# Gated cross-attention with an FFN on one core: where the FFN's weight pieces stand in the first batch

## The reference, cut to what matters

```python
q = _qdq(x) @ _qdq(wq).T + bq                  # x is layernorm(x); 16 heads of 32
kv = cond @ wkv.T + bkv
attn = softmax(einsum('bnhd,bmhd->bhnm', q, k) * scale)
o = einsum('bhnm,bmhd->bnhd', attn, v)
x = x + tanh(g_xattn) * (_qdq(o) @ _qdq(wp).T + bp)

def _quantized_matmul(x, w, scale):
    wq = w.astype(float8_e4m3fn).astype(x.dtype)
    return einsum('bsi,io->bso', x, wq) * scale
fuse = silu(_quantized_matmul(h, gate_w, gate_scale)) * _quantized_matmul(h, up_w, up_scale)
x = x + tanh(g_ffn) * _quantized_matmul(fuse, down_w, down_scale)   # h is layernorm(x)
```

## Time and profile before

| | |
|---|---|
| median of three runs | 920.49 us |
| the profiled execution | 921.14 us, its span 919.3 us |
| TensorE busy | 856.7 us, 93% |
| VectorE busy | 674.4 us, 73% |
| ScalarE busy | 554.2 us, 60% |
| POOL busy | 249.3 us, 27% |
| chain that ended last | TensorE 66%, VectorE 16%, issue 8%, ScalarE 7%, DMA 1%, POOL 1% |

### The profile page before, as it was taken

One profiled execution on the slowest core, in us unless ns is written; L12 is line 12 of the kernel. 1 busy time (PEld: TensorE's weight loads), 2 busy tenths in 40 slices (PEclk: granted clock), 3 DMA queues, 4 the chain that ended last, 5 costly groups with the idle time before them and its releaser, 6 DMA issues.

```text
span 919.3 us, 13602 instructions
## 1 busy us (share of the span) xinstructions
PE 856.7 (93%) x4968; PEld 316.1 (34%) x4976; DVE 674.4 (73%) x1306; ACT 554.2 (60%) x737; POOL 249.3 (27%) x236
## 2 busy tenths in 40 slices
PE   5989989997999999999899999999999989998998
PEld 2422212244433332224443332224433322234444
DVE  6888956988676779968676678986867778788222
ACT  5547978752456559873456649884356779862230
POOL 1145755875127600001017700002002210020230
PEclk9999999999899999999999999999999999999899
DMA  9334333221201133200111133300010023200001
GB/s 331 105 87 133 95 112 91 75 89 46 52 24 47 44 124 98 52 1 1 26 50 35 42 112 99 78 2 1 9 44 1 1 61 102 53 1 30 5 1 46
DMA packets 37251, 55.29 MB, mean 60 GB/s; under 512 B 8960, under 2 KB 15424, under 8 KB 37184
## 3 DMA queue, kind: packets, MB, share of 16 engines
q1 hardware_dynamic: 35264, 48.13, 18.4%
q0 software_dynamic: 1920, 6.29, 2.3%
HBM read 31.21 MB, written 4.19 MB: 39 GB/s over the span
## 4 chain that ended last, share of the span: by engine, by line
PE 66%; DVE 16%; issue 8%; ACT 7%; DMA 1%; POOL 1%; SPq 0%; ACTq 0%; DVEq 0%; POOLq 0%
PE ps L1389 32%; PE ps L1577 8%; PE ps L1540 7%; PE ps L1557 7%; DVE acc L1119 4%; ACT r L877 4%; PE ps L1512 4%; PE ps L1571 3%; PE ps L1585 1%; PE ps L1373 1%; DVE kst L1094 1%; DVE am L974 1%; DVE r L1261 1%; DVE vv L1186 1%; DVE xq L1094 1%
## 5 line engine op out<-in xcount | busy, mean ns | idle before, releaser
L877 ACT ACTIVATE r<-ps 128x1024 f32<-128x1024 f32 (+1 forms) x300 | 253.3, 901 | 59.6 <-PE ps L1540 57.2
L1094 DVE CUSTOM_DVE_ANT_0 kst<-ps,kst 128x512 f32<-128x512 f32 x192 | 124.5, 685 | 30.3 <-PE ps L1512 28.4
L1540 PE MATMUL ps<-qst,kst 97*128 97x512 f16 x512 | 138.7, 385 | 7.4 <-DMA qst<-crow 4.7
L1557 PE MATMUL ps<-r,vv 128*32 128x512 f32 x1024 | 138.1, 612 | 3.3 <-ACT r L877 3.2
L1119 DVE TENSOR_TENSOR acc<-acc,r 128x1024 f32<-128x1024 f32 x120 | 138.6, 1216 | 0.0
L834 ACT ACTIVATE kst<-ps 128x1024 f32<-128x1024 f32 x96 | 98.2, 1023 | 53.3 <-PE ps L1445 53.0
L1389 PE MATMUL ps<-xs,w_gate 128*128 128x512 f16 x384 | 92.6, 385 | 1.5 <-DVE xs L1306 1.5
L1389 PE MATMUL ps<-xs,w_up 128*128 128x512 f16 x384 | 91.2, 380 | 0.0
L1540 PEld LDWEIGHTS ps<-qst,kst 97*128 97x128 f16 x512 | 40.4, 97 | 145.0 <-ACT r L877 86.7
L932 ACT ACTIVATE qst<-ps,gs_c 128x512 f32<-128x512 f32 x48 | 33.0, 688 | 69.4 <-PE ps L1389 69.4
L1335 DVE SCALAR_TENSOR_TENSOR xq<-ps,us_c,qst 128x512 f32<-128x512 f32 x48 | 36.0, 749 | 52.3 <-PE ps L1389 52.3
(11 more groups left out here) (166 smaller groups left out, 1286.1 us busy)
## 6 DMA issues: line engine op xcount, KB each, us to landing
kst<-k_reg SPq DMA_DIRECT2D x192, 64.0 KB
qst<-q_reg SPq DMA_DIRECT2D x192, 32.0 KB
xs<-in_x SPq DMA_DIRECT2D x4, 1024.0 KB, 5.9
cf<-in_ctxT POOLq DMA_DIRECT2D x16, 256.0 KB, 3.5
xres<-in_x SPq DMA_DIRECT2D x3, 1024.0 KB, 5.1
out<-xres SPq DMA_DIRECT2D x12, 256.0 KB, 2.0
acc<-in_down_w SPq DMA_DIRECT2D x10, 256.0 KB, 2.7
vv<-in_wkvT SPq DMA_DIRECT2D x2, 1024.0 KB, 9.8
```

The lines of the kernel that those rows point to most:

```text
L877: nc.scalar.activation(prob[:, s:s + heads, :], ps[:, first_bank:first_bank + heads, :], ACT.Exp, scale=SCALE).then_inc(exp_done, 1)
L1094: ins = nc.vector.tensor_tensor_reduce(kept(b, n)[:, k, :], bank(PAIR + k), kept(b, n)[:, k, :], 1.0, -3.0e38, ALU.add, ALU.max, mx[:, g % ...
L1540: mm = nc.tensor.matmul(bank(first_bank + k), kst[0:97, g % 2, j + k, t * P:(t + 1) * P], qst[0:97, g % 2, j + k, :], start=True, stop=True)
L1557: mm = nc.tensor.matmul(ps[j * DH:(j + 1) * DH, O_BANK, :], vv[:, t, h * DH:(h + 1) * DH], prob[:, p_slot(b, u, j), :], start=(t == 0), st ...
```

## The change

Three pieces instead of six stand after value tiles: those after V2, V3 and V4. Units 15, 17 and 19 take one each, so that 27 stand in the units. Of the six late ones, the pair after V1 to V3 (L1275) moves behind the low half of K0. POOL follows: its chunks stand behind pieces 4, 6, ..., 18 instead of 7, 9, ..., 21, which from unit 16 on are earlier units (16, 18, 20 for 18, 21, 23); the inverse deviation stands behind piece 14, again that of unit 16; two pieces instead of four are rounded before the second inverse deviation, four after it. SP loads fewer pieces before each row and stack.

```diff
-W_EARLY, W_LATE = MT - len(EARLY_V), 6
+W_EARLY, W_LATE = 3, 6
-W_CHAIN = 4
-W_NONE = (3, 6, 9, 11, 13, 15, 17, 19)
+W_CHAIN = 2
+W_NONE = (3, 6, 9, 11, 13)
-W_VARIANCE = 16
+W_VARIANCE = 14
...
-W_AHEAD = {"keys1": 5, "shift0": 8, "queries1": 10, "shift1": 13, "stack2": 15, "shift2": 20, "stack3": 20,
-           "shift3": 24, "residual": 30}
-W_STACK = {2: (15, 16, 16, 16, 17, 17), 3: (20, 21, 21, 21, 21, 23)}
+W_AHEAD = {"keys1": 5, "shift0": 7, "queries1": 7, "shift1": 11, "stack2": 13, "shift2": 15, "stack3": 17,
+           "shift3": 23, "residual": 30}
+W_STACK = {2: (13, 13, 13, 13, 13, 13), 3: (17, 17, 17, 18, 19, 21)}
...
-            stack(qst, (qhi, qlo, qhi), 1, (9, 9, W_AHEAD["queries1"]))
+            stack(qst, (qhi, qlo, qhi), 1, (0, 0, W_AHEAD["queries1"]))
...
                 v_tile(a_full, a_count(f"V{n}"), A_BANK[f"V{n}"], a_free, n)
-                w_magnitudes()
+                if n < len(EARLY_V) + W_EARLY:
+                    w_magnitudes()
...
                 late_magnitudes(2)
                 next_v(1, 2, 3)
-                late_magnitudes(2)
...
                         k_low(b + 1, n, d_bank(b, f"K{n}"), d_free)
+                        late_magnitudes(2 * (n == 0))
```

## The result

The changed kernel takes **911.34 us** (median of 4 runs, 910.51 to 912.61); the kernel before, run beside it on the same chip, 920.83 (919.34 to 921.73). The ratio is 0.990, 95% interval 0.988 to 0.992: faster by 9.5 us. Forecast were 911.8 and a gain of 8.7. The profiled execution took 911.59 us, span 909.8, so it stands for the median. In the session of the first four experiments one run of the kernel before took 3535.54 us; it is left out of the medians and ratios here.

What follows compares the result with a forecast made beforehand. The chain is mostly TensorE's own work, so gains come only where it waits. Units 2.7 plus step 6.0 make 8.7 us off the median 920.49: 911.8 us, chance 0.60, range 908.0 to 916.0.

Steps and rivals of the forecast that it cites:

- Unit 16: Batch 0, unit 16: the row of maxima leaves SP at 127.3; TensorE's 3.87 us wait and 1.57 slow clock go, 5.44.
- Unit 24: Batch 0, unit 24: the row, ready at 159.4, lands just in time; TensorE's 0.86 us wait goes.
- Rival C: Slower: unit 24's row held behind piece 22's load, if POOL is 8.9 us later than summed; 921.5 or more, chance 0.04.
- Units 17 to 22: Batch 0: POOL is full, so new waits for maxima cost 4.0 us; units end 2.7 earlier, values' products included.
- The term of unit 21: Batch 0, unit 21: TensorE loses 0.7 us, carried on from the inverse deviation POOL delivers late in unit 17.
- rival A: Units 17 to 22: the new waits, hanging on one late deviation, don't come; gain 12.7, 907.8 us, chance 0.15.
- the 188.8 to 189 named as a sign: End of batch 0's units: they would be over near 188.8-189 us in the trace.
- Values' products: Batch 0: pieces 3, 4, 5 leave the places after V5, V6, V7; only V5's is on the path, gain 0.34 us.
- The step: Batch 0 to 1, first value product to matmuls behind K2's first difference: 46.5 us, 6.0 less than 52.49.
- The 1.0 for the key difference: Step, pieces 34 and 35 after K0's low half: the key difference TensorE wants is held by POOL, 0.4 to 1.0 us.
- The 0.2 for pieces 32 and 33: Step, after the normalisation: their 2.2 us stand against 2.03 us that VectorE waited for ScalarE, cost 0.2.
- from K3 on nothing changes: After the step: no change from K3 on, with TensorE continuous; no gain or loss summed there.

Runs made afterwards that it cites:

- the first four experiments: The units alone, the step alone, the row held and the early deviation: four edited kernels, measured 916.57, 915.25, 915.13 and 911.48 us.
- the row held: Changed kernel, but SP loads 17 pieces instead of 15 before the row of maxima of group 2; 915.13 us, ratio 0.9941.
- the early deviation: Changed kernel, with POOL computing the inverse deviation behind piece 13 (unit 15) instead of 14; 911.48 us, ratio 0.9907.
- the pair at K2: Changed kernel, with pieces 34 and 35 ahead of K2's low half instead of behind K0's; 909.52 us, ratio 0.9896.
- the units alone: Changed kernel, with pieces 32 and 33 back behind tiles V1 to V3 and four pieces before the second inverse deviation; 916.57 us, ratio 0.9957.
- the step alone: Kernel before, with only the pair after V1 to V3 moved behind K0's low half, two pieces before the second inverse deviation; 915.25 us, ratio 0.9938.
- the pieces spread: The pair at K2, plus pieces of units 17 and 19 moved to 11 and 13, deviation, chunks and SP's counts fitted; 908.18 us, ratio 0.9874.

## Why the prediction came out right

**Unit 16.** Right in cause and size. The row left at 127.80 for the 127.3 summed, TensorE did not wait, and the clock stayed up; the row held by two loads brings both back. Here the Trainium skill (TensorE: Matmul & The Clock Gate, "Part 1: The HAM clock gate") says that the slow clock is the default and that a monitor sets the clock by how busy TensorE has been of late. The trace agrees so far: after stops of 3.69 to 3.87 us at unit 16 the granted clock was 0.50 in all four profiles that have them. The length of a stop alone does not decide: after 1.76 us in the step it was 0.50 in one profile of five, after 2.55 us in the last batch in six of ten.

**Unit 24.** Right: no wait for its row, though its issue came at 161.00 where 159.4 was summed. TensorE was nearly as much later itself. It was close: the weight load of the first scores stood 0.8 us for the row, beside matmuls. Rival C needed far more.

**Units 17 to 22.** The mechanism was right, one size not. Summed were 2.1, 0.7 and 1.2; measured 2.02, 1.19 and 1.21. The term of unit 21 was too small by 0.5. I had derived it from the late deviation, and the held row and the early deviation both show that it does not hang on that. Nor do the three waits together hang on one late deviation, as rival A had it. All in all the stretch was 2.02 us shorter for the 2.7 forecast: 0.4 of the miss is the longer waits, the rest is not placed. With the start-up 0.37 us longer, the next batch's first product came at 190.17, not at the 188.8 to 189 named as a sign.

**Values' products.** Right: the wait behind V5 was 0.43 us for 0.76 (68.17 in the changed kernel), 0.33 for the 0.34 forecast.

**The step.** Right: 46.67 us for 46.5. The 1.0 for the key difference, which I took over 0.4 because a row showed VectorE holding POOL up, measured 0.84 (the stop of 1.76 less 0.92), and the pair at K2 gave 1.0 back. The 0.2 for pieces 32 and 33 is 0.3 at most: with the pair at K2 the step takes 45.66 us for the 45.33 of the next batch. By the Trainium skill (SBUF — State Buffer, "SBUF: two separate sides") the difference, with two inputs from SBUF, has to wait while an operation of POOL that reads SBUF holds the pair of ports that they share. The trace agrees: 1.05 us for 0.68 beside POOL's rounding, and POOL's next operation, at 235.74, took 1.60 us for 1.16.

**The last batch.** Not in the prediction at all. I wrote that from K3 on nothing changes, and the work did not; its time did. TensorE stands 2.55 us for the second normalisation in all ten profiles. In the kernel before the granted clock falls behind this stop, in the changed kernel it does not. The windows of before:

```profile
849.62:850.62 1.00, 1.00 (x6) 0.67 (x4) 1.00 (x3) 0.62 (x2) 0.00 (x0) 0.50 0.66 250
853.62:854.62 1.00, 1.00 (x3) 0.30 (x2) 0.00 (x0) 0.00 (x0) 0.00 (x0) 0.50 0.00 0
```

And of the changed kernel:

```profile
844.13:845.13 1.00, 0.79 (x4) 0.41 (x5) 0.06 (x1) 0.00 (x0) 0.00 (x0) 1.00 0.00 0
848.13:849.13 1.00, 1.00 (x7) 0.43 (x5) 0.61 (x1) 0.00 (x0) 0.00 (x0) 1.00 0.00 0
```

Without these 2.05 us the gain would have been 7.5 for the 8.7 summed: I was 1.2 too high on what I reasoned about (0.7 in the units, 0.2 in the step, and the start-up's 0.37), and the total hides it. That the forecast of 911.8 lies within 0.5 of the result is luck; with the last batch as before the time would have been near 913.4, still inside the range.

## What stays open

Why the last batch's clock goes one way in one kernel and the other way in the next. In ten profiles of eight kernels the work of that stretch is the same, and it takes 92.66 and 92.67 us (the kernel before, twice), 91.7 (the row held), 91.6 (the units alone), 91.5 (the step alone), 91.4 (the deviation early) and 90.6 (the changed kernel twice, the pair at K2, the pieces spread). What differs is the granted clock behind the 2.55 us stop. In the kernel before it is 0.50 from 850 to 855 us, through the turns of the normalised rows (L1373) and into the 192 matmuls. In the four with 91.4 to 91.7 us it is 0.50 in those turns alone, 16 matmuls that take 3.2 to 3.5 us where they take 1.94 at full clock, and the 192 take 41.60 as in the changed kernel. In the other four it does not fall. The chain of the units alone:

```profile
844.27 3.46 PE ps L1374 x16
849.21 41.60 PE ps L1390 x192
```

What decides it I can't say, and the time at which the stop comes does not alone: in the second profile of the changed kernel and in that of the early deviation the same piece of it begins at 833.31 and 833.24, and the stretches took 90.60 and 91.37. I did not try to shift that batch alone, and more profiles of one kernel would be needed to tell the kernel's part from chance.

## What to carry to other kernels

Where one queue issues everything in order, what stands ahead of an urgent transfer is part of its price: two loads too many cost 3.2 us in their own stretch and 3.8 in all. Before moving work to an engine that seems idle in a stage, add up all that its new neighbours already have there; the same 27 pieces made TensorE wait 4.4 us in one arrangement and 1.7 in another. And a gain from the clock can arrive in a stretch that the change never touches, so compare stretches, not totals.

## What I had not expected of the hardware

The lower clock of the last batch (granted 0.50) repeated in two profiles of each kernel: 92.66 and 92.67 us against 90.61 and 90.60 for the same stretch of work. After stops of the same length (1.76 us ahead of K2's first difference) the 12 matmuls took 2.70 us in the changed kernel and 4.30 in the one with the row held.
